# The first group's input moves to a buffer of its own, the second group's input is loaded early, the start's loads are split over two queues, and the order of all steps is found anew

## The reference, cut to what matters

```python
# tokenizer
x = jnp.einsum('bchpwq,dcpq->bhwd', xp, patch_w) + patch_b     # 64 patches per image, D = 192
x = _layernorm(x.reshape(B, -1, D), ln_g, ln_b) + _sinusoidal_pe(N, D)
identity = x
x = sparse_attn(ff(x)) + identity
x = ff(x) + x
# the rest
h = jnp.concatenate([h, txt], axis=1)
h = h + _L0_attn_ref(_layernorm(h, axis=-1), ...)   # x + _ssm(ln(x)); + attn(ln(x)); + ffn(ln(x))
h = h + _L0_ffn_ref(_layernorm(h, axis=-1), ...)    # q, k normed per head, softmax, gates, projection
```

## Time and profile before

| | us |
|---|---|
| median of 3 runs | 673.8 (671.29 to 675.58) |
| profiled execution, its own time | 679.45 |
| its span, first to last instruction | 677.7 |
| PE (TensorE matmul) busy | 578.7 (85%) |
| DVE (VectorE) busy | 435.3 (64%) |
| ACT (ScalarE) busy | 293.1 (43%) |
| POOL (GpSimd) busy | 59.3 (9%) |
| mean granted TensorE clock | 0.919 of full speed |

### The profile page before, as it was taken

The page is one execution under the profiler, slowest core; times in us unless marked ns, Lnnn a source line. Parts: engine busy times, 40 slices in busy tenths (PEclk is TensorE's granted clock), DMA queues, the critical chain, the costliest instruction groups (busy, mean ns, idle before and its releaser), DMA issues.

```text
span 677.7 us, 10708 instructions
## 1 busy us (share of the span) xinstructions
PE 578.7 (85%) x4137; PEld 405.6 (60%) x4137; DVE 435.3 (64%) x879; ACT 293.1 (43%) x392; POOL 59.3 (9%) x56
## 2 busy tenths in 40 slices
PE   4600999898888989999998999999996889999786
PEld 3400865674656766566776776577584564774465
DVE  4000356776984488488684675787863978865983
ACT  0200154436342255465561454574733456542553
POOL 0000123000021003020101012021000020010000
PEclk9655899999599799999997899999997899998989
DMA  4598000100000000010000000000000000000000
GB/s 113 151 224 235 1 1 1 54 1 6 1 1 1 0 2 1 1 48 2 6 1 20 1 1 2 0 1 1 1 1 18 1 1 0 2 1 18 0 1 18
DMA packets 13442, 16.01 MB, mean 24 GB/s; under 512 B 6683, under 2 KB 10958, under 8 KB 13006
## 3 DMA queue, kind: packets, MB, share of 16 engines
q1 hardware_dynamic: 11790, 14.12, 8.0%
q10 hardware_dynamic: 1600, 1.18, 0.5%
HBM read 14.11 MB, written 1.18 MB: 23 GB/s over the span
## 4 chain that ended last, share of the span: by engine, by line
issue 38%; PE 32%; DVE 12%; SPq 8%; POOL 5%; ACT 4%; DMA 1%; POOLq 0%; ACTq 0%; DVEq 0%
PE ps L643 8%; SPq L554 5%; PE ps L647 5%; PE ps L919 3%; PE ps L977 3%; PE ps L742 2%; DVE smax L1576 2%; DVE pr L1578 2%; POOL side_wide L1798 2%; PE ps L967 1%; DVE psum L1587 1%; DMA x_in<-in_xT 1%; DVE pr L1599 1%; PE ps L702 1%; PE ps L801 1%
## 5 line engine op out<-in xcount | busy, mean ns | idle before, releaser
L1576 DVE TENSOR_REDUCE smax<-ps 96x12 f32<-96x1152 f32 x32 | 43.2, 1349 | 29.6 <-PE ps L967 19.0
L702 PE MATMUL ps<-side_in,x_in 128*128 128x192 f32 x96 | 21.9, 396 | 43.1 <-DMA x_in<-in_xT 43.1
L1253 ACT ACTIVATE pr<-pr 96x1152 f32<-96x1152 f32 x28 | 32.6, 1163 | 45.7 <-DVE pr L1578 45.7
L702 PEld LDWEIGHTS ps<-side_in,x_in 128*128 128x128 f32 x96 | 20.2, 238 | 45.0 <-issue 39.5
L643 PE MATMUL ps<-w_cqkv,side_c 128*128 128x512 f32 (+1 forms) x102 | 44.9, 571 | 1.2 <-DVE pr L1578 1.2
L977 PE MATMUL ps<-w_ident,pr 96*96 96x96 f32 x336 | 35.3, 259 | 7.8 <-DVE pr L1599 6.2
L1386 DVE TENSOR_TENSOR a_emb<-ps,w_patch_b 128x384 f32<-128x384 f32 x3 | 1.7, 558 | 61.9 <-PE ps L702 61.9
L1259 ACT ACTIVATE pT<-ps 96x1152 f32<-96x1152 f32 x28 | 31.5, 1125 | 20.5 <-PE ps L977 20.4
L977 PEld LDWEIGHTS ps<-w_ident,pr 96*96 96x96 f32 x336 | 30.2, 132 | 15.0 <-issue 6.1
L1587 DVE TENSOR_REDUCE psum<-pr 96x12 f32<-96x1152 f32 x28 | 37.5, 1341 | 2.2 <-ACT pr L1253 2.2
L1578 DVE TENSOR_TENSOR pr<-ps,smax 96x1152 f32<-96x1152 f32 x28 | 37.9, 1353 | 1.0
(11 more groups left out here) (363 smaller groups left out, 1307.1 us busy)
## 6 DMA issues: line engine op xcount, KB each, us to landing
x_in<-in_xT SPq DMA_DIRECT2D x3, 768.0 KB, 4.7
b_kB<-in_cqkv SPq DMA_DIRECT2D x1, 1152.0 KB
w_cqkv<-in_cqkv SPq DMA_DIRECT2D x2, 567.0 KB
w_cqkv<-in_cqkv SPq DMA_DIRECT2D x1, 864.0 KB
out<-side_c ACTq DMA_DIRECT2D x3, 288.0 KB, 2.3
x_in<-in_xT SPq DMA_DIRECT2D x3, 256.0 KB, 4.5
side_in<-in_patchT SPq DMA_DIRECT2D x3, 192.0 KB, 3.4
side_tff<-in_tok_ff SPq DMA_DIRECT2D x1, 576.0 KB, 6.7
```

Source lines behind the costliest of these rows:

```text
L702: m = pe.matmul(t[:, tile * D:(tile + 1) * D], x_in[:, j, tile * 128:(tile + 1) * 128], w_patch[:, j, :], start=(j == 0), stop=(j == KP - 1))
L1253: act.activation(w.y.pr[:, s % 2, :], w.y.pr[:, s % 2, :], ACT.Exp, scale=head ** -0.5)\
L1576: dve.tensor_reduce(mx, t, AX.X, ALU.max).then_inc(w.S[stage + "_sub"], 1)
```

## The change

The diff has four parts. First, SP's loads are split: ScalarE issues the three parts of the first input, the four `v_split` loads, the twelve bias rows and the sixteen pieces of `w_tqkv`; SP issues the rest, with `w_tff1` sooner and the sixteen pieces of `w_qkv` last. Second, the first input gets a buffer of its own, `e_x_in`, cut from `heads`, which the mixer's heads use later. Third, the input of group 1 is loaded to `x_in` behind `w_tff2`, with no wait. Since `b_oT` lies in `heads`, its row of ones is set later, in `a_wc.1`, and `b_pr` waits for it. Fourth, all three lists are new (a line of each is shown).

```diff
 STEPS_TEXT = {
     "pre": """
-    d_en d_em d_x0=7 warm.51=3 a_bc=5 a_en d_f1.0=2 a_em=5 d_f2.0=1 d_h2.0 a_tb=5 a_x0=0 d_qk=3 a_f1.0=5 d_e.0 d_s.0
-    d_v=4 a_f2.0 d_s.1=5 d_pt.0=1 a_h2.0=4 d_o.0=3 d_e.1 d_pt.1=1 a_qk d_ot.0 a_wc.0 d_o.1=3 d_ot.1=3 a_e.0 d_pr
+    d_em=1 d_en d_x0=6 warm.0=7 a_bc d_f1.0=5 a_em a_en d_f2.0 d_h2.0 a_tb=7 a_x0 d_qk a_f1.0 d_s.0=0 a_f2.0=5
+    a_wc.0 d_e.0 d_v=1 d_s.1 d_pt.0 a_h2.0 d_o.0 d_e.1 d_pt.1=2 a_qk d_ot.0=2 d_o.1=1 d_ot.1=5 a_pb d_pr=1 a_s.0=4
...
     "post": """
-    b_u.1=2 b_qk=4 warm b_s.0=2 b_s.1 b_n.0 b_e.0 b_e.1 e_u=1 b_v b_pt.0 b_n.1 b_s.2=1 b_o.0=7 b_pt.1 b_s.3=4 b_e.2
+    e_u=1 b_u.1=5 e_g e_qk.0 b_qk e_v.0=1 b_s.0 b_e.0 b_s.1=0 b_v=6 b_e.1 b_n.0 e_qk.1 e_v.1=0 b_pt.0=4 b_o.0=5
...
+        e_x_in, = cut(heads, (KP, TA))
...
         @block.sync
         def _(sp):
             for part in range(3):
                 j = slice(2 * part, 2 * part + 2)
                 sp.dma_start(w_patch[:, j, :], patchT[:, j]).then_inc(loads[f"patch{part}"], 16)
-                sp.dma_start(x_in[:, j, :], xT[0, :, j]).then_inc(loads[f"patch{part}"], 16)
...
-            bias_rows_of("tok_", tok_ff1, tok_qkv)
-            bias_rows_of("", ffn1, qkv)
-            split_rows("tff1", w_tff1, tok_ff1)
+            split_rows(sp, "tff1", w_tff1, tok_ff1)
             sp.dma_start(w_tff2[:], tok_ff2).then_inc(loads["tff2"], 16)
-            split_rows("tqkv", w_tqkv, tok_qkv, cols=HEAD_PARTS)
+            sp.dma_start(x_in[:, :, :], xT[1]).then_inc(S["x_in"], 16)
...
             sp.dma_start(w_cproj[:, :, :], cproj).then_inc(loads["cproj"], 16)
+            split_rows(sp, "qkv", w_qkv, qkv, cols=HEAD_PARTS)
...
             def a_em(w, _):
-                if w.chain == "d":
-                    return
-                if w.section == "pre":
-                    sp.wait_ge(S["early_" + filled("a_em")], upto("early_" + filled("a_em"), 0))
-                else:
+                if w.section == "loop":
                     sp.wait_ge(w.S[filled("a_em")], w.upto(filled("a_em"), w.a - 1))
                     sp.wait_ge(w.S[filled("c_qt")], w.upto(filled("c_qt"), w.c - 1, 2))
-                sp.dma_start(x_in[:, :, :], xT[w.group]).then_inc(w.S["x_in"], 16)
+                    sp.dma_start(x_in[:, :, :], xT[w.group]).then_inc(w.S["x_in"], 16)
...
         @block.scalar
         def _(act):
+            for part in range(3):
+                j = slice(2 * part, 2 * part + 2)
+                act.dma_start(e_x_in[:, j, :], xT[0, :, j]).then_inc(loads[f"patch{part}"], 16)
...
+            act.wait_ge(s_pad, 1)
+            bias_rows_of(act, "tok_", tok_ff1, tok_qkv)
+            bias_rows_of(act, "", ffn1, qkv)
+            split_rows(act, "tqkv", w_tqkv, tok_qkv, cols=HEAD_PARTS)
             act.wait_ge(s_set, 1)
             act.wait_ge(loads["vec"], 16 * n_loads["vec"])
```

More of the change, by code:

```diff
@@ L75 @@
-    b_o.0=5 b_e.2 b_pt.1=3 b_e.3 a_cv.0 b_n.2 b_s.3=1 a_cv.1 b_o.1 b_pt.2 b_n.3 a_in.1 b_o.2 b_pt.3=4 a_cv.2
-    b_pr.0=0 a_gt.0 b_pr.1=3 a_gt.1 b_o.3=1 a_gt.2 b_pr.2=2 a_out.0 b_u.2 a_out.1=1 b_f1.0=5 b_f1.1=0 a_wc.3
-    a_out.2=3 b_f2.0 b_f2.1 b_f2.2=2 warm.52=7
+    d_em=1 d_en d_x0=6 warm.0=7 a_bc d_f1.0=5 a_em a_en d_f2.0 d_h2.0 a_tb=7 a_x0 d_qk a_f1.0 d_s.0=0 a_f2.0=5
+    a_wc.0 d_e.0 d_v=1 d_s.1 d_pt.0 a_h2.0 d_o.0 d_e.1 d_pt.1=2 a_qk d_ot.0=2 d_o.1=1 d_ot.1=5 a_pb d_pr=1 a_s.0=4
+    a_wc.1 d_f1.1=0 a_s.1=6 d_f2.1 a_e.0 a_e.1 d_h2.1 a_pt.0 d_ht a_v=0 a_o.0=0 a_pt.1=1 d_u=6 a_wc.2 a_ot.0=3
@@ new lines @@
+    a_o.1=1 d_in.0=3 a_ot.1=1 d_cv.0 a_pr=2 d_in.1=5 d_cv.1 d_cv.2 d_gt.0 d_gt.1 a_f1.1 d_gt.2 d_out.0=3 d_out.1
+    d_out.2=6 a_f2.1=3 a_h2.1=0 b_u.1 a_ht=3 b_qk=0 a_u b_s.0=1 warm.1=6 b_s.1=5 b_e.0 b_e.1 b_n.0 a_in.0 b_n.1
+    b_pt.0=4 b_s.2=1 b_v b_e.2 a_cv.0 b_o.0=7 b_pt.1=4 b_n.2 b_s.3=0 b_o.1 b_e.3 b_pt.2=5 a_cv.1 a_in.1 b_n.3
+    b_o.2=4 b_pt.3=1 a_cv.2 a_gt.0 b_pr.0 b_pr.1=7 a_gt.1 b_o.3 a_gt.2 b_pr.2 a_out.0=2 b_u.2 a_out.1 b_f1.0
+    b_f1.1=1 a_wc.3 a_out.2=5 b_f2.0=7 b_f2.1=6 b_f2.2=1
@@ L78 @@
     """,
     "loop": """
[L80 to L84, removed]
@@ L85 @@
-    c_n.2 a_in.0 a_in.1=0 c_o.1 a_cv.0 c_v.3 c_n.3 c_pt.2=1 a_gt.0 a_cv.1 c_pr.0=0 c_o.2=3 c_pt.3=0 a_cv.2 a_gt.1
-    c_pr.1=5 c_o.3 a_gt.2 a_out.0 a_out.1 a_out.2 c_pr.2
+    c_u=5 b_u.1=1 c_g=7 b_qk=3 a_em=7 a_en b_s.0 b_v a_x0=3 b_e.0 b_s.1 b_e.1 a_f1.0 b_pt.0 b_n.0 b_n.1 a_f2.0=7
+    b_s.2=0 a_h2.0 b_o.0=3 b_e.2 b_n.2 b_pt.1=2 a_qk b_s.3 b_o.1 b_pr.0=4 b_pt.2=0 b_e.3 a_s.0 b_n.3 a_e.0 b_o.2=3
+    a_v=7 a_pt.0=0 a_s.1=4 b_pt.3 a_e.1 a_o.0=6 b_pr.1=0 a_pt.1=4 b_o.3=7 a_ot.0=1 a_o.1=4 c_qk.0 a_ot.1 c_qk.1
@@ L90 @@
[L90 to L94, removed]
@@ L527, in _ @@
                 sp.dma_start(w_patch[:, j, :], patchT[:, j]).then_inc(loads[f"patch{part}"], 16)
-                sp.dma_start(x_in[:, j, :], xT[0, :, j]).then_inc(loads[f"patch{part}"], 16)
             sp.sem_inc(S["early_x_in"], 16)
[L530 to L534, removed]
+            sp.dma_start(w_patch_b[:], patch_b).then_inc(loads["vec"], 16)
@@ L540, in rows_and_bias @@
[L540 to L555, removed]
@@ L569, in text @@
-            def text(group, done):
-                for rows, part, src_rows, src_part in ((slice(0, HC), 0, slice(0, HC), 0),
-                                                       (slice(HC, 128), 0, slice(0, 128 - HC), 1),
-                                                       (slice(0, 64), 1, slice(128 - HC, HC), 1)):
-                    sp.dma_start(hT[rows, part, :, NI:N], txtT[group, src_rows, src_part]).then_inc(done, 16)
-            HEAD_PARTS = ((0, 0, D), (D, D + 128, 64), (D + 64, D, 128), (2 * D, 2 * D, D))
@@ L1336, in _ @@
             dve.memset(hx[:, :, :], 0.0).then_inc(s_heat, 1)
-            for t in (e_oT, a_oT, b_oT):
+            for t in (e_oT, a_oT):
                 dve.memset(t[HC:HC + 1, 0, :], 1.0)
@@ L1719, in a_wc @@
                     dve.tensor_tensor(w_cqkv[:, 1, :], w_cqkv[:, 1, :], last_row[:, :], ALU.subtract).then_inc(s_less, 1)
+                    dve.wait_ge(S["early_" + filled("a_em")], upto("early_" + filled("a_em"), 0))
+                    dve.memset(b_oT[HC:HC + 1, 0, :], 1.0).then_inc(s_ones, 1)
                 else:
```

88 lines of the change are left out of this document (59 added, 29 removed).

## The result

The changed kernel takes 647.1 us (median of 4 runs, 644.3 to 653.6) beside 672.5 us before (4 runs, 670.9 to 675.6): a ratio of 0.963, 95% interval 0.9547 to 0.9713. The forecast was 631.6 us with a range of 619 to 643, so the time lies 4 us above the range: faster, but by 25 us and not by 42. On another chip the same pair gave 646.8 and 674.8 us, ratio 0.9583 (0.9543 to 0.9624).

What follows compares the result with a forecast made beforehand. PE was taken as the bound almost everywhere, except a 38.0 us wait for the late-issued `x_in`. Start 39.2 us (42.5 less 3.3), plus 4, less 1, gave 42.2 us: 637.2, or 631.6 us for the median, range 619 to 643.

Steps and rivals of the forecast that it cites:

- `a_em` starts at 24.9 instead of 67.37 us: 42.5 us: Start: loading group 1's input earlier removes PE's 38.0 us wait, and 4.5 us more come from the beginning.
- correction of 5.65 us for the long profile: Sum: the profiled execution of 679.45 us lay 5.65 us above the median run, so that was taken off.
- Stall: 3.3 us: Before `d_pt.1`: VectorE waits at `a_wc.0` for `w_cproj`, in at 52 us, holding PE 3.3 us; range none to 6.8.
- The order. ... I take 4 us: Start of post: the new list fills 8.0 us idle and 5.1 us of clock; gain 4 us, ends 0 and 11.
- 1 us of loss: Pre behind the start, and loop: new lists shift steps and add a `warm` to the loop; 1 us lost.
- The work taken from later leaves holes there: Post: a reason, beside chain b starting 7 us later, for taking 4 us and not all 13 us.
- 10 us worse over two passes: Pre and loop lists: the bad bound, an idle time as large again; the good bound was 8 us better.
- The order gives part back: Rival: holes in loop and pre as large again, 10 to 15 us, time 644 us; chance 0.07.
- The transfers are the wall: Rival: rate stays near 195 GB/s, `w_cproj` in at 62 us, stall 13 us, time 641 us; chance 0.15.
- The slow case: Rival: new banks in loop and post make PE wait at each softmax unit; 682 us at 1.8 us each; chance 0.02.
- the full ring: Start, ScalarE's 35 more issues: free unless its ring fills; then 7 us more, just using up the 7 us cover.
- 2.5 us at the very start: Start: fewer loads ahead on SP's queue make `x0T` ready at 17.1 us instead of 19.62.

Runs made afterwards that it cites:

- `a_wc.0` later: Changed kernel with `a_wc.0` moved behind `d_ot.0`: 639.9 us; the same with the old lists for loop and post: 634.6 us.
- gates apart: Changed kernel, gate weights loaded behind `cqkv` under their own count, which `a_wc.0` awaits instead of `w_cproj`: 641.9 us; with old loop and post lists also, 635.4 us.
- one queue: Changed loads with three old lists, but SP issues every load: 645.5 us; the same with SP's counts given before its loads: 646.1 us.

## Why the prediction was wrong

**Right: what the load's place was worth.** "So `a_em` starts at 24.9 instead of 67.37 us: 42.5 us." The trace has 24.61. With the old lists, whose `a_wc.0` stands later, no stall is to be taken off, and the step gives 673.8 - 42.5 = 631.3 us; measured were 630.1, 629.3 and 629.0 on two chips. Here the correction of 5.65 us for the long profile held too. Beside the kernel before in their own groups these are 45.1 to 45.7 us, some 3 more than 42.5, which nothing in the sum names. In the profiles the first `c_u` comes 43 us sooner in the mean (173.3 to 180.0 us in four, 219.1 and 220.3 before).

**Right in place, too small in price: "Stall: 3.3 us".** The wait for `w_cproj` came where and when it was said. But PE came to `d_pt.1` at 52.7 us, not at 55.1, and VectorE to its wait at 46.6, not at 49.1, so that PE waited 5.7 us (8.4 in another run), and then had the lower clock (0.89 from 60 to 70 us). Moving `a_wc.0` was worth 6.9 us on one chip; taking `w_cproj` out of its wait 7.1 on another (646.4 less 639.3, both with the old post). The lead of 39.25 us at `d_pt.1` was right because PE was early by as much as it then waited longer.

**Wrong: "The order. ... I take 4 us" and "1 us of loss".** This is the step that failed, in sign. The sum had 4 us gained in post, 1 us lost in the other two lists, together +3; what the three lists cost, by medians, is

| step | us |
|---|---|
| old lists (mean of three medians) | 629.5 |
| new list before the mixers, `a_wc.0` later | 634.6: +5.1 |
| new lists in loop and post too | 639.9: +5.3 |
| `a_wc.0` where the new list has it | 646.8: +6.9 |

That is 17.3 us, of which the prediction had 3.3 as the stall, and it gave 3 back: 631.6 + 3.6 + 5.1 + 5.3 + 3 is 648.6, against 647.1 measured. The chips of the rows differ, and scatter of 2 us is in each. On one chip alone the steps are 629.3, 635.4 (new list before the mixers, gates apart), 639.9 and 646.8 us: 6.1, 4.5 and 6.9, in all 17.5. Of the 4.5 to 5.3 us of loop and post, the loop's list has most: 4.1 us with the gates apart, while that of post cost 2.7 there and 0.4 with the gates in their old place (both across chips).

Where the argument on post went wrong is seen in the windows. It counted the idle time and low clock of the first 28.2 us as something to recover. They were recovered (2.9 us idle of 27.7, clock 1.00), and lost again 30 us later, where VectorE is busy 84% and more of the time; in sum post brought 0 to -3 us where 4 were taken. "The work taken from later leaves holes there" was in the text, priced at nothing certain; the lower end of post's own range, 0, is about what came. Larger is what was taken for 1 us: a list with the same steps in other places cost 5 to 6 us before the mixers, and the loop's list 4 (none of them in its first pass), 9 to 10 in all. The prediction had named "10 us worse over two passes" as a bound and put none of it into the sum. Why the new places cost that is shown only in part: 1 to 3 us of idle time before the mixers, otherwise a lower clock.

**The rivals.** "The order gives part back" (644, chance 0.07) is the case that came, helped by the larger stall, and deserved several times that chance: all three lists are written anew, and nothing in the trace of before spoke for their being better. "The transfers are the wall" had the weight 8 to 10 us too late (62 us; 52.5 and 53.9 measured). The slow case's banks don't show: the loop's first pass is 141.6 us. The pieces of `w_tqkv` on ScalarE cost nothing visible: it had issued them all by 18.9 us, in 9.9 us. Why some issues of SP take long (15.33 us for 16 pieces in the earlier trace rows, 3.8 us for `w_cproj` alone here, against 0.4 to 0.6 for one load otherwise) no run shows; the full ring that the prediction names is a guess.

**The second queue.** The Trainium skill, "DMA: Bandwidth & Descriptors", section "Issuing engines are not separate DMA queues", says that several issuers save only issue time, and that this is usually small beside the transfer. The profiles fit the mechanism: `w_cproj` takes as long from issue to landing with one queue as with two and is only issued later. They don't fit the size: with one issuer the DMA engines have a share of 0.47 in the first 20 us and with two 0.82, and the runs are 15 us apart. The prediction drew too little from it: apart from 2.5 us at the very start it gave the second queue no price.

## What to carry to other kernels

When a hole of 38 us is closed, the next late thing can be read from the trace of before to within 2 us (`w_cproj` at 52 said, 52.5 and 53.9 measured), but the price of its wait must include the clock that PE has afterwards. An order found anew is a change by itself: run it apart before it is taken together with another; here the loads with the old lists are 2.7% faster than the change as made. Where the DMA engines are half idle at the start of a kernel, look at how long the issuing engine takes for each small load.

## What the runs showed of the hardware that was not expected

- Medians of one kernel in three groups on two chips agreed within 1.1 us (630.1, 629.3, 629.0), but its single runs lay up to 9 us apart (626.8 to 636.2). The two profiles of the kernel before had spans of 677.7 us at a mean granted clock of 0.919 and 670.0 us at 0.936.
- Taking a wait away need not save it: with one queue 11.0 us of VectorE's waiting for SP's late counts became 13.0 us for `w_cproj` at the next step, and the time stayed the same (645.5 and 646.1 us).
- An earlier start of VectorE bought nothing against a transfer: in the two profiles of the changed kernel `w_cproj` came in at 52.5 and 53.9 us, and the wait for it was 5.9 and 8.6 us.
